# A linear-attention layer with key dimensions innermost, normalisation on GpSimd, biases as matmul rows, and its weights loaded in the layer before

## The chip, the cores and the metric

The kernel runs on one core of a Trainium2 chip. A core has a matrix engine (TensorE, "PE" in rows; its weight loads are "PEld"), VectorE ("DVE"), ScalarE ("ACT"), GpSimd ("POOL") and SyncE ("SP"), which here only issues transfers. Engines run their own instruction streams in order and wait for each other through semaphores. The metric is the device time of one execution in microseconds, lower is better. Before the change the median of 3 runs is 1361.99 us (1359.45 to 1362.17).

## The reference

Four layers over a sequence of 2048 rows of 128 floats, each added to x after a layer norm: softmax attention (16 heads), a layer of 8 experts with one expert per row, the linear attention that is edited here, and the expert layer once more. The linear attention:

```python
qkv = x @ w_qkv.T + b_qkv                   # x: layer-normed, (1, 2048, 128)
q, k, v = heads(qkv)                        # 16 heads of 8
q_prime, k_prime = elu(q) + 1, elu(k) + 1
kv_cumsum = cumsum(einsum('bhtd,bhte->bhtde', k_prime, v), axis=2)
context = einsum('bhtd,bhtde->bhte', q_prime, kv_cumsum)
norm = einsum('bhtd,bhtd->bht', q_prime, cumsum(k_prime, axis=2))
out = context / (norm[..., None] + 1e-6)
x = x + out @ w_out.T + b_out
```

## The kernel before, in words

x stays on the chip as 16 tiles of 128 rows (one row of the sequence per partition). The four layers are written one behind the other: `attention`, `ffn`, `linear_attention`, `ffn`. Each is one block with a barrier at its end, and its own PSUM and SBUF tiles.

`linear_attention` treats one tile per step. For tile t: normalise (`xn`, L1051, VectorE), transpose on TensorE (L1153) and copy by ScalarE (`xT`, L1098); one product gives q, k and v in PSUM (`z`, L1159), and a second one with a single row, `b_row` by `ones` in f32, adds the bias (L1160). ScalarE and VectorE make elu+1 of q and k (`qk`; "features", L1102, L1105, L1063); v with a column of ones behind each head is `v1`. GpSimd writes out the outer product of k and v1 for every row (`outer`, L1037: 16 heads x 8 key dimensions x 9 values = 1152 floats), TensorE sums it over the rows of the tile so far with a triangular matrix (`sums`, L1143, three products of 512, 512 and 128 columns). VectorE multiplies by q (`prod`, L1059) and sums over the 8 key dimensions (`own`, L1066). The order of the 1152 floats is head, key dimension, value, so that sum reads with a step of 9 floats.

What lies before the tile comes through a state. TensorE forms k^T v of the tile (`delta`, L1135), ScalarE copies it (`mine`, L1095), GpSimd masks it to the heads (`fresh`, L1027) and adds it to the running `state` (L1031); q^T against the state is `inter` (L1148). VectorE adds `inter` and `own` (`tot`, L1069), adds 1e-6 (L1071), takes the reciprocal (L1073) and multiplies (`o`, L1075). `o` is transposed (L1165), copied (`oT`, L1108), multiplied by the output weights (L1126) and added to x (L1056). The output bias is added to x earlier, by GpSimd (L1024). Buffers are doubled (U = 2).

Each engine's order is written out by `skewed`: at step n it emits its stages for tiles n - offset, in the order in which the table names them. TensorE: y (5), qT (2), z (1), xT (0), sums (2), oT (4). VectorE: norm (0) and y (5), heads (3), features (1), sums (2). The middle of it is a hardware loop with two tiles a turn. GpSimd: bias (0), outer (1), state (2). Weights and biases are loaded at the start of the layer (L995 to L998), transposed on TensorE (L1116, L1117) and copied (L1086).

`ffn` computes the expert of every row, gives the rows places sorted by expert, scatters them to memory by 16 indirect transfers that GpSimd issues (L720), and then goes through 24 slots of 128 rows. TensorE and VectorE stand still while the scatter is issued.

## Time and profile before

| | us |
|---|---|
| median of 3 runs | 1361.99 |
| the profiled execution | 1360.53 |
| its span | 1358.8 |
| attention, first expert layer up to its end | 0 to 1127.1 |
| linear attention | 1127.1 to 1246.4 |
| second expert layer | 1246.4 to 1358.8 |

| engine | busy us | share of the span |
|---|---|---|
| TensorE | 1173.5 | 86% |
| VectorE | 957.3 | 70% |
| ScalarE | 794.6 | 58% |
| GpSimd | 829.2 | 61% |

Busy shares are means over four layers with different limits, so for the linear layer its own stretch has to be read. A row "start, duration, engine, line, operation, out<-in" is one instruction or several merged ones (xN); in brackets stands how long the engine was idle before it and what it waited for. Matrix products in f32 run as several passes and show as x2. PEclk is the clock that TensorE was granted, as a share of 2.4 GHz.

### The profile page before, as it was taken

To read this page: it belongs to the slowest core of one execution; us is meant where nothing else is said; L and a number is where in the kernel's file an instruction comes from. 1 tells how busy PE (TensorE), PEld (TensorE's weight loads), DVE (VectorE), ACT (ScalarE), POOL (GpSimd) and SP (SyncE) were. 2 spreads that over 40 slices of the span, in tenths; PEclk is the share of its full clock that TensorE was granted. 3 is DMA by queue.
4 is the path that set the end of the run, shared out by engine and by line. 5 is a ranking of instruction groups with operands and counts; after the bars stand their busy time and mean duration, and the time that the engine had idled before them with its cause. 6 is when DMAs were issued, how large, how long until landed. Compare 5 with 4: busy or idle time off the path is not lost. (4 is left out here: it accounts for less than half of the span.)

```text
span 1358.8 us, 24424 instructions
## 1 busy us (share of the span) xinstructions
PE 1173.5 (86%) x7936; PEld 855.3 (63%) x7936; DVE 957.3 (70%) x2108; ACT 794.6 (58%) x2192; POOL 829.2 (61%) x813
## 2 busy tenths in 40 slices
PE   5999999999999999999999999999973585885285
PEld 4666667676767767676676667676753582443285
DVE  5878677867776786878677777867743355998254
ACT  6777576767757775766677576766721342322053
POOL 0675668757866775887576768757852443552433
PEclk9899999999999999999999999999995796998588
DMA  4950200200020011002000200200000221000023
GB/s 124 125 141 16 48 1 1 52 12 1 1 63 1 1 32 32 1 1 63 1 1 8 57 1 1 50 14 1 1 1 17 57 61 32 1 0 1 29 60 98
DMA packets 52689, 41.18 MB, mean 30 GB/s; under 512 B 14177, under 2 KB 41442, under 8 KB 52578
## 3 DMA queue, kind: packets, MB, share of 16 engines
q1 hardware_dynamic: 50018, 34.50, 11.9%
q0 software_dynamic: 2560, 5.26, 1.2%
q8 instruction: 62, 1.02, 0.3%
q14 instruction: 49, 0.40, 0.1%
HBM read 13.49 MB, written 9.48 MB: 17 GB/s over the span
## 5 line engine op out<-in xcount | busy, mean ns | idle before, releaser
L325 POOL TENSOR_SCALAR at_prob<-at_prob,at_scale 128x512 f32<-128x512 f32 (+1 forms) x480 | 656.2, 1383 | 5.6
L353 DVE TENSOR_REDUCE at_nmax<-at_ps 128x1 f32<-128x512 f32 (+3 forms) x640 | 375.9, 603 | 154.1 <-PE at_ps L519 150.5
L434 ACT ACTIVATE at_prob<-at_ps,at_nmax 128x512 f32<-128x512 f32 (+3 forms) x640 | 393.1, 623 | 44.6 <-DVE at_nmax L353 43.7
L530 PE MATMUL at_ps<-ident,at_prob 128*128 128x128 f32 x2176 | 328.7, 275 | 23.4 <-DVE at_probT L376 19.1
L530 PEld LDWEIGHTS at_ps<-ident,at_prob 128*128 128x128 f32 x2176 | 255.7, 140 | 110.5 <-issue 52.6
L516 PE MATMUL at_ps<-at_k_st,at_q_parts 128*128 128x512 f32 (+3 forms) x640 | 285.1, 445 | 6.1 <-ACT at_prob L434 3.6
L448 ACT ACTIVATE at_probT<-at_ps 128x512 f32<-128x512 f32 (+1 forms) x288 | 165.1, 573 | 212.2 <-PE at_ps L530 188.0
L545 PE MATMUL at_ps<-at_probT,at_v 128*64 128x256 f32 (+1 forms) x2304 | 270.1, 374 | 12.3 <-DVE at_probT L376 12.3
L519 PE MATMUL at_ps<-at_k_st,at_q_parts 128*128 128x512 f32 (+3 forms) x640 | 253.1, 396 | 0.0
L376 DVE COPY at_probT<-at_ps 128x512 f32<-128x512 f32 (+1 forms) x288 | 189.0, 656 | 68.1 <-PE at_ps L530 64.7
L545 PEld LDWEIGHTS at_ps<-at_probT,at_v 128*64 128x64 f32 x2304 | 155.2, 136 | 107.1 <-issue 48.5
L516 PEld LDWEIGHTS at_ps<-at_k_st,at_q_parts 128*128 128x128 f32 x640 | 122.2, 191 | 46.7 <-ACT at_prob L434 22.0
L434 ACT ACTIVATION_READ_ACCUMULATOR at_prob<-at_ps,at_nmax 128x1 f32 x640 | 131.1, 205 | 0.0
L519 PEld LDWEIGHTS at_ps<-at_k_st,at_q_parts 128*128 128x128 f32 x640 | 125.8, 197 | 1.3
L382 DVE TENSOR_SCALAR at_prob<-at_prob,at_scale 128x512 f32<-128x512 f32 (+1 forms) x160 | 93.0, 583 | 2.5 <-POOL at_scale L318 2.0
L727 POOL DMA_INDIRECT slots_out<-f_ys,f_back x48 | 47.2, 984 | 63.9 <-DVE f_ys L836 49.2
L866 ACT ACTIVATE f_hT<-f_ps,f_wfix 128x128 f32<-128x128 f32 x192 | 54.6, 370 | 34.1 <-PE f_ps L911 28.8
L306 POOL TENSOR_TENSOR at_gap<-at_low,at_nmax 128x8 f32<-128x8 f32 (+2 forms) x48 | 9.9, 206 | 93.8 <-DVE at_low L358 93.8
L720 POOL DMA_INDIRECT slots_in<-f_xn,f_pos_u x32 | 31.3, 980 | 55.7 <-DVE f_pos_u L811 46.6
L904 PE MATMUL f_ps<-ident,f_xs 128*128 128x128 f32 x48 | 14.2, 296 | 57.3 <-DMA f_xs<-slots_in 57.3
L1037 POOL TENSOR_TENSOR li_outer<-li_qk,li_v 128x1152 f32<-128x1152 f32 x16 | 35.5, 2220 | 44.1 <-DVE li_qk L1063 44.1
L316 POOL COPY at_scale<-at_rinv 128x4 f32<-128x4 f32 x16 | 3.0, 189 | 96.6 <-DVE at_rinv L364 96.6
(189 smaller groups left out, 1364.1 us busy)
## 6 DMA issues: line engine op xcount, KB each, us to landing
at_q_parts<-at_q_parts SPq DMA_DIRECT2D x64, 256.0 KB, 3.5
f_xs<-slots_in SPq DMA_DIRECT2D x48, 64.5 KB
slots_in<-zeros SPq DMA_DIRECT2D x2, 1536.0 KB, 19.4
wall<-in_L_ffn_w_dram SPq DMA_DIRECT2D x1, 2048.0 KB, 19.8
wall<-in_L_ffn_w_dram SPq DMA_DIRECT2D x4, 512.0 KB, 6.1
f_got<-slots_out SPq DMA_DIRECT2D x8, 256.0 KB, 3.6
out_dram<-x SPq DMA_DIRECT2D x4, 256.0 KB, 2.4
slots_out<-f_ys,f_back POOLq DMA_INDIRECT x48
```

Of the source, the lines that this page charges most:

```text
L325: pool.tensor_scalar(cols, cols, scale[:, k, u, c:c + 1], None, ALU.mult).then_inc(s_fix["pool"], 1)
L353: dve.tensor_reduce(nmax[:, j % 2, u % 4, c:c + 1], bank, AX.X, ALU.max, negate=True).then_inc(s_max, 1)
L376: dve.tensor_copy(probT[1][n % TURNED][:, 0:w], turn_ps[1][:, 0:w]).then_inc(s_probT[1], 1)
L382: dve.tensor_scalar(cols, cols, scale[:, k, u, c:c + 1], None, ALU.mult).then_inc(s_fix["dve"], 1)
L434: act.activation(prob[j % 2][u % 4][:, c * BANK:c * BANK + w], ring[use_of["score", p, u, c] % RING][:, 0:w], ACT.Exp, bias=nmax[:, j % 2, ...
L448: act.activation(probT[0][n % TURNED][:, 0:w], turn_ps[0][:, 0:w], ACT.Copy).then_inc(s_probT[0], 1)
L516: pe.matmul(bank[:, 0:w], q_hi[h][:, r * P:(r + 1) * P], keys, start=True, stop=False)
L519: pe.matmul(bank[:, 0:w], q_lo[h][:, r * P:(r + 1) * P], keys, start=False, stop=True).then_inc(s_score, 1)
L530: last = pe.transpose(turn_ps[h][:, b * P:(b + 1) * P], prob[j % 2][2 * i + h][:, t * P:(t + 1) * P], ident[:, :])
L545: last = pe.matmul(z_ps[part_of, to:to + w], v[:, t, part_of], probT[h][group(p, j, g) % TURNED][:, 2 * P * b:2 * P * b + w], start=t == 0 ...
L727: pool.indirect_dma_start(scratch_out[:, :], bass.IndirectOffsetOnAxis(ap=back[k][:, :], axis=0), ys[k][:, :], None).then_inc(s_store[k], 16)
L866: last = act.activation(hT[k][:, f, :], ps[2 + c % 2][:, f * P:(f + 1) * P], ACT.Gelu, bias=wfix[k][:, B1.start + f:B1.start + f + 1])
```

## The change

1. The outer product and `prod` are laid out head, value, key dimension: the 8 key dimensions are innermost, and the sum over them reads neighbours.
2. The normalisation moves from VectorE to GpSimd; GpSimd's addition of the output bias goes.
3. The output bias and the 1e-6 become extra products with a row of ones. All bias rows are held as F32R in two parts, the rounded value in row 0 and what the rounding lost in row 32 of a tile of 33 rows (`b_rows`), against `ones` of 33 rows; the rows between are zero. The z bias goes the same way.
4. The running sum of the state is kept in PSUM form: `past` = k^T v + identity x `mine` of the tile before. GpSimd only masks it (one instruction in place of two).
5. xT, qT and oT share one PSUM bank (`turn_ps`), with waits so that none is written while another is read; `past`, `inter` and `out` have banks of their own.
6. Loads, masks and transposed weights are made by `linear_setup` inside the first expert layer (`beside`), into tiles that stay.
7. The steps are written out straight, without the hardware loop; buffers are guarded by explicit waits.

VectorE, one step in the middle of the linear layer, before (`li_prod` the product with q, `li_own` the sum over key dimensions, `li_xn` the normalised tile, `li_qk` the features):

```order
L1051 TENSOR_SCALAR li_xn<-x,li_mv,li_rstd 128x128
L1056 TENSOR_TENSOR x<-li_yp,x 128x128
L1066 TENSOR_REDUCE li_own<-li_prod 128x144
L1069 TENSOR_TENSOR li_tot<-li_stp,li_own 128x144
L1071 TENSOR_SCALAR li_den<-li_tot 128x16
L1073 RECIPROCAL li_den<-li_den 128x16
L1075 TENSOR_TENSOR li_o<-li_tot,li_den 128x128
L1063 SCALAR_TENSOR_TENSOR li_qk<-li_zp,li_ex 128x256
L1059 TENSOR_TENSOR li_prod<-li_sums,li_qk 128x1152
```

and after:

```order
L1114 TENSOR_TENSOR x<-li_outp,x 128x128
L1128 TENSOR_REDUCE li_own<-li_prod 128x144
L1131 TENSOR_TENSOR li_tot<-li_interp,li_own 128x144
L1133 RECIPROCAL li_den<-li_tot 128x16
L1137 TENSOR_TENSOR li_o<-li_tot,li_den 128x128
L1125 SCALAR_TENSOR_TENSOR li_qk<-li_zp,li_ex 128x256
L1118 TENSOR_TENSOR li_prod<-li_sums,li_qk 128x1152
```

The normalisation and the addition of 1e-6 are gone; nothing else has moved.

TensorE, one step, before (`li_yp` holds oT and the output product, `li_stp` is `inter`):

```order
L1126 MATMUL li_yp<-li_wT,li_oT 128x128
L1131 MATMUL li_qTp<-ident,li_qk 128x128
L1159 MATMUL li_zp<-li_wT,li_xT 128x384
L1160 MATMUL li_zp<-li_b_row,li_ones 128x384
L1153 MATMUL li_xTp<-ident,li_xn 128x128
L1135 MATMUL li_qTp<-li_v,li_qk 128x144
L1143 MATMUL li_sums<-li_outer,li_upto 128x512 x2
L1143 MATMUL li_sums<-li_outer,li_upto 128x128
L1148 MATMUL li_stp<-li_state,li_qT 128x144
L1165 MATMUL li_yp<-ident,li_o 128x128
```

and after (`li_turnp` is the shared bank of the transposes):

```order
L1249 MATMUL li_zp<-li_wT,li_xT 128x384
L1250 MATMUL li_zp<-li_b_rows,li_ones 128x384
L1243 MATMUL li_turnp<-ident,li_xn 128x128
L1222 MATMUL li_pastp<-li_v,li_qk 128x144
L1224 MATMUL li_pastp<-li_mine,ident 128x144
L1232 MATMUL li_sums<-li_outer,li_upto 128x512 x2
L1232 MATMUL li_sums<-li_outer,li_upto 128x128
L1238 MATMUL li_interp<-li_state,li_qT 128x144
L1239 MATMUL li_interp<-li_b_rows,li_ones 128x144
L1254 MATMUL li_turnp<-ident,li_o 128x128
L1211 MATMUL li_outp<-li_wT,li_oT 128x128
L1212 MATMUL li_outp<-li_b_rows,li_ones 128x128
```

Three products are new (L1224, L1239, L1212); the order of the others is as before (qT, L1216, stands right ahead of the piece shown).

GpSimd, the first steps, before:

```order
L1037 TENSOR_TENSOR li_outer<-li_qk,li_v 128x1152
L1024 TENSOR_TENSOR x<-x,li_bo_all 128x128
L1037 TENSOR_TENSOR li_outer<-li_qk,li_v 128x1152
L1027 TENSOR_TENSOR li_fresh<-li_mine,li_block_mask 128x144
L1031 TENSOR_TENSOR li_state<-li_state,li_fresh 128x144
L1024 TENSOR_TENSOR x<-x,li_bo_all 128x128
L1037 TENSOR_TENSOR li_outer<-li_qk,li_v 128x1152
L1027 TENSOR_TENSOR li_fresh<-li_mine,li_block_mask 128x144
```

and after:

```order
L1103 TENSOR_TENSOR li_outer<-li_qk,li_v 128x1152
L1086 TENSOR_SCALAR li_xn<-x,li_mv,li_rstd 128x128
L1103 TENSOR_TENSOR li_outer<-li_qk,li_v 128x1152
L1092 TENSOR_TENSOR li_state<-li_mine,li_block_mask 128x144
L1086 TENSOR_SCALAR li_xn<-x,li_mv,li_rstd 128x128
L1103 TENSOR_TENSOR li_outer<-li_qk,li_v 128x1152
L1092 TENSOR_TENSOR li_state<-li_mine,li_block_mask 128x144
L1086 TENSOR_SCALAR li_xn<-x,li_mv,li_rstd 128x128
L1103 TENSOR_TENSOR li_outer<-li_qk,li_v 128x1152
```

The normalisation of tile n+1 stands behind the outer product of tile n and the state of tile n-1.

The diff, cut to its core:

```diff
@@ ffn
             def _(sp):
                 sp.dma_start(wred[:, :], w_red).then_inc(s_gin, 16)
                 sp.dma_start(wg[:, :], w_g).then_inc(s_wg, 16)
+                if beside:
+                    beside["sync"](sp)
                 sp.wait_ge(s_scat, 16 * NT)
...
             def _(pool):
                 pool.iota(xn[:, :, D:D + 1].bitcast(U32), pattern=[[P, NT], [0, 1]], base=0, channel_multiplier=1).then_inc(s_ids, 1)
+                if beside:
+                    beside["gpsimd"](pool)
...
                 dve.tensor_scalar(slot_e[:, :], slot_f[:, :], float(E - 1), None, ALU.min).then_inc(s_slot, 1)
+                if beside:
+                    beside["vector"](dve)
...
                 act.activation(ex[:, :, :], sub[:, :, :], ACT.Exp).then_inc(s_ex, 1)
+                if beside:
+                    beside["scalar"](act, ps[3])
...
+                if beside:
+                    pe.wait_ge(beside["tensor"](pe, ps[3]), 1)
@@ linear_setup (new)
+    def on_sync(sp):
+        sp.dma_start(w_nat[:, 0:3, :], w_qkv.rearrange("(a p) d -> p a d", p=P)).then_inc(s_in, 16)
+        sp.dma_start(w_nat[:, 3, :], w_out).then_inc(s_in, 16)
+        sp.wait_ge(s_clear, 3)
+        for r in (0, BROWS - 1):
+            sp.dma_start(b_nat[r:r + 1, 0:3 * D], b_qkv.unsqueeze(0)).then_inc(s_bias, 16)
+            sp.dma_start(b_nat[r:r + 1, 3 * D:4 * D], b_out.unsqueeze(0)).then_inc(s_bias, 16)
+    def on_vector(dve):
+        dve.wait_ge(s_c, 3)
+        dve.tensor_copy(ones[:, :], ones_f[:, :])
+        dve.wait_ge(s_bias, 64)
+        dve.wait_ge(s_clear, 3)
+        dve.tensor_copy(b_cut[:, :], b_nat[:, :]).then_inc(s_cut, 1)
+        dve.tensor_copy(b_rows[0:BROWS - 1, :], b_nat[0:BROWS - 1, :])
+        dve.wait_ge(s_cut, 1)
+        row = slice(BROWS - 1, BROWS)
+        dve.tensor_tensor(b_rows[row, :], b_nat[row, :], b_cut[row, :].bitcast(F32), ALU.subtract).then_inc(s_const, 1)
+    def on_tensor(pe, bank):
+        pe.wait_ge(s_in, 32)
+        for a in range(4):
+            last = pe.transpose(bank[:, a * P:(a + 1) * P], w_nat[:, a, :], ident[:, :])
+        last.then_inc(s_wTp, 1)
+        return s_wT
...
@@ linear_attention, GpSimd
+                    if stage == "norm":
+                        if t >= U:
+                            pool.wait_ge(s_xTp, t - U + 1)
+                        pool.tensor_scalar(xn[k][:, :], x[:, t, :], mv[:, t, 0:1], rstd[:, t:t + 1],
+                                           ALU.subtract, ALU.mult).then_inc(s_xn, 1)
...
-                        pool.tensor_tensor(state[k][:, :], state[1 - k][:, :], fresh[k][:, :], ALU.add).then_inc(s_state, 1)
+                        pool.tensor_tensor(state[k][:, :], mine[k][:, :], block_mask[:, :, :].rearrange("p h e -> p (h e)"),
+                                           ALU.mult).then_inc(s_state, 1)
...
-                        kk = qk[k][:, D:2 * D].rearrange("p (h d) -> p h d", d=DL).unsqueeze(3).to_broadcast([P, HL, DL, DL + 1])
-                        vv = v1[k][:, :, :].unsqueeze(2).to_broadcast([P, HL, DL, DL + 1])
+                        kk = qk[k][:, D:2 * D].rearrange("p (h d) -> p h d", d=DL).unsqueeze(2).to_broadcast([P, HL, DL + 1, DL])
+                        vv = v1[k][:, :, :].unsqueeze(3).to_broadcast([P, HL, DL + 1, DL])
                         pool.tensor_tensor(outer[k][:, :, :, :], kk, vv, ALU.mult).then_inc(s_outer, 1)
@@ VectorE
-                        dve.tensor_reduce(own[:, :, :], prod[:, :, :].rearrange("p (h d) e -> p h e d", d=DL), AX.X, ALU.add).then_inc(s_own, 1)
+                        dve.tensor_reduce(own[:, :, :], prod[:, :, :, :], AX.X, ALU.add).then_inc(s_own, 1)
...
-                        dve.tensor_scalar(den[:, :].unsqueeze(2), tot[:, :, DL:DL + 1], EPS, None, ALU.add).then_inc(s_den, 1)
-                        dve.wait_ge(s_den, t + 1)
-                        dve.reciprocal(den[:, :], den[:, :]).then_inc(s_rden, 1)
+                        dve.reciprocal(den[:, :].unsqueeze(2), tot[:, :, DL:DL + 1]).then_inc(s_rden, 1)
@@ TensorE
+                        pe.matmul(out, oT[k][:, :], wT[:, 3, :], start=True, stop=False)
+                        pe.matmul(out, ones[:, :], b_rows[:, 3 * D:4 * D], start=False, stop=True).then_inc(s_out, 1)
...
+                        last = pe.matmul(past, qk[k][:, D:2 * D], v1[k][:, :, :].rearrange("p h e -> p (h e)"), start=True, stop=t == 0)
+                        if t:
+                            last = pe.matmul(past, ident[:, :], mine[1 - k][:, :], start=False, stop=True)
+                        last.then_inc(s_past, 1)
...
+                            pe.matmul(inter, qT[k][:, :], state[1 - k][:, :], start=True, stop=False)
+                        pe.matmul(inter, ones[:, :], b_rows[:, 4 * D:4 * D + VX], start=t == 0, stop=True).then_inc(s_inter, 1)
...
-                        pe.matmul(z_ps[:, 0:3 * D], ones[:, :], b_row[:, :], start=False, stop=True).then_inc(s_z, 1)
+                        pe.matmul(z_ps[:, 0:3 * D], ones[:, :], b_rows[:, 0:3 * D], start=False, stop=True).then_inc(s_z, 1)
```

## Rows read from the trace of the kernel before

**Rows 1.** Table of stretches: us, busy us of each engine, granted clock, DMA.
```profile
1041.70:1065.50 23.80, 0.02 (x1) 0.02 (x1) 0.77 (x1) 0.00 (x0) 15.68 (x16) 0.50 0.16 49
1134.00:1147.50 13.50, 12.09 (x21) 5.16 (x22) 1.10 (x3) 2.78 (x11) 5.80 (x5) 0.50 0.00 0
1158.00:1239.00 81.00, 68.26 (x246) 35.20 (x246) 77.81 (x119) 23.32 (x87) 46.54 (x52) 0.98 0.00 0
```
**Rows 2.** Timeline, VectorE, one step: start us, duration us, what.
```profile
1190.26 1.35 DVE L1059 TENSOR_TENSOR li_prod<-li_sums,li_qk 128x1152 f32<-128x1152 f32 x1
1191.52 1.20 DVE L1051 TENSOR_SCALAR li_xn<-x,li_mv,li_rstd 128x128 f32 x1
1192.64 0.28 DVE L1056 TENSOR_TENSOR x<-li_yp,x 128x128 f32 x1
1192.85 2.21 DVE L1066 TENSOR_REDUCE li_own<-li_prod 128x144 f32<-128x1152 f32 x1
1195.16 0.31 DVE L1069 TENSOR_TENSOR li_tot<-li_stp,li_own 128x144 f32<-128x144 f32 x1
1195.50 0.17 DVE L1071 TENSOR_SCALAR li_den<-li_tot 128x16 f32<-128x16 f32 x1
1195.71 0.25 DVE L1073 RECIPROCAL li_den<-li_den 128x16 f32<-128x16 f32 x1
1196.20 0.42 DVE L1063 SCALAR_TENSOR_TENSOR li_qk<-li_zp,li_ex 128x256 f32<-128x256 f32 x1
```
**Rows 3.** Timeline, TensorE, the same step and the next y.
```profile
1190.23 0.49 PE L1126 MATMUL li_yp<-li_wT,li_oT 128*128 128x128 f32 x2 [0.37 <-ACT li_oT L1108]
1190.66 0.82 PE L1159 MATMUL li_zp<-li_wT,li_xT 128*128 128x384 f32 x2
1191.41 0.91 PE L1160 MATMUL li_zp<-li_b_row,li_ones 1*128 1x384 f32 x2
1192.78 0.33 PE L1153 MATMUL li_xTp<-ident,li_xn 128*128 128x128 f32 x1 [0.46 <-DVE li_xn L1051]
1193.20 2.10 PE L1143 MATMUL li_sums<-li_outer,li_upto 128*128 128x512 f32 x6
1195.52 0.51 PE L1148 MATMUL li_stp<-li_state,li_qT 128*128 128x144 f32 x2 [0.22 <-DVE li_tot L1069]
1195.87 0.27 PE L1165 MATMUL li_yp<-ident,li_o 128*128 128x128 f32 x1
1196.51 0.49 PE L1126 MATMUL li_yp<-li_wT,li_oT 128*128 128x128 f32 x2 [0.37 <-ACT li_oT L1108]
```
**Rows 4.** Line of the normalisation: count, ns minimum/median/maximum, first and last start.
```profile
L1051 DVE TENSOR_SCALAR li_xn<-x,li_mv,li_rstd x16: 337/1198/1204, 1132.1 to 1222.9; 128x128 f32<-128x128 f32 x8, 128x128 f32 x8
```
**Rows 5.** Timeline, GpSimd, the same step.
```profile
1190.42 2.22 POOL L1037 TENSOR_TENSOR li_outer<-li_qk,li_v 128x1152 f32<-128x1152 f32 x1 [2.56 <-DVE li_qk L1063]
1193.17 0.49 POOL L1031 TENSOR_TENSOR li_state<-li_state,li_fresh 128x144 f32<-128x144 f32 x1
```
**Rows 6.** Timeline, TensorE in the attention layer, an F32R product and its successor.
```profile
701.18 0.40 PE L519 MATMUL at_ps<-at_k_st,at_q_parts 128*128 128x512 f32 x1
701.42 0.60 PE L530 MATMUL at_ps<-ident,at_prob 128*128 128x128 f32 x4
```
**Rows 7.** Groups by line and shape, 300 to 1000 us: count, busy us, mean ns.
```profile
L325 POOL TENSOR_SCALAR at_prob<-at_prob,at_scale 128x128 f32<-128x128 f32 x46 | 27.5, 598 | 0.0
```
**Rows 8.** Timeline, the start of the linear layer: first transpose, first sums, second product.
```profile
1134.05 0.45 PE L1153 MATMUL li_xTp<-ident,li_xn 128*128 128x128 f32 x1 [3.10 <-ACT li_wT L1086]
...
1143.49 4.05 PE L1143 MATMUL li_sums<-li_outer,li_upto 128*128 128x512 f32 x6
...
1152.81 1.35 DVE L1059 TENSOR_TENSOR li_prod<-li_sums,li_qk 128x1152 f32<-128x1152 f32 x1
```
**Rows 9.** Timeline, the last product of the linear layer.
```profile
1238.08 1.35 DVE L1059 TENSOR_TENSOR li_prod<-li_sums,li_qk 128x1152 f32<-128x1152 f32 x1
```
**Rows 10.** Timeline, GpSimd, first scatter of the first expert layer.
```profile
1041.76 1.18 POOL L720 DMA_INDIRECT slots_in<-f_xn,f_pos_u  x1 [22.26 <-DVE f_pos_u L811]
```

More of the change, by code:

```diff
@@ L620, in static_tile, with ffn @@
     return c if isinstance(turn, int) else None
-def ffn(nc, shp, keep, tag, w_red, w_g, scratch_in, scratch_out, has_stats, out=None):
+def ffn(nc, shp, keep, tag, w_red, w_g, scratch_in, scratch_out, has_stats, out=None, beside=None):
     T, D, NT, NC, TPC = shp.T, shp.D, shp.NT, shp.NC, shp.TPC
@@ L934, in linear_attention @@
+def linear_attention(nc, shp, keep):
     D, NT = shp.D, shp.NT
@@ L1016, in _ @@
[L1016 to L1031 removed]
+                    pool.memset(v1[k][:, :, DL:DL + 1], 1.0).then_inc(s_one, 1)
@@ L1107, in emit @@
                         act.wait_ge(s_oTp, t + 1)
+                        if t >= U:
+                            act.wait_ge(s_out, t - U + 1)
                         act.activation(oT[k][:, :], oT_ps, ACT.Copy).then_inc(s_oT, 1)
-                skewed(act, NT, U, {"qT": 2, "z": 1, "xT": 0, "delta": 2, "oT": 4}, emit)
+                in_turn({"qT": 2, "z": 1, "xT": 0, "past": 2, "oT": 4}, emit)
             @block.tensor
             def _(pe):
-                pe.wait_ge(s_in, 32)
-                for a in range(3):
-                    pe.transpose(sums_ps[:, a * P:(a + 1) * P], w_nat[:, a, :], ident[:, :])
@@ L1127, in emit @@
                     elif stage == "qT":
                         pe.wait_ge(s_qk, t + 1)
-                        if not first(turn, c):
-                            pe.wait_ge(s_dcopy, t)
-                        pe.transpose(qT_ps[:, 0:P], qk[k][:, 0:D], ident[:, :]).then_inc(s_qTp, 1)
+                        turn_bank_free(t, "q")
+                        pe.transpose(qT_ps, qk[k][:, 0:D], ident[:, :]).then_inc(s_qTp, 1)
                     elif stage == "sums":
                         pe.wait_ge(s_v, t + 1)
-                        pe.wait_ge(s_qT, t + 1)
@@ L1137, in emit @@
+                        last.then_inc(s_past, 1)
                         pe.wait_ge(s_outer, t + 1)
-                        if not first(turn, c):
+                        if t:
                             pe.wait_ge(s_prod, t)
-                        flat = outer[k][:, :, :, :].rearrange("p h d e -> p (h d e)")
+                        flat = outer[k][:, :, :, :].rearrange("p h e d -> p (h e d)")
                         for a in range(0, OUTER, BANK):
@@ L1144, in emit @@
                         last.then_inc(s_sums, 1)
[L1145 removed]
+                        pe.wait_ge(s_qT, t + 1)
+                        if t:
                             pe.wait_ge(s_tot, t)
                             pe.wait_ge(s_state, t)
[L1148 removed]
+                            pe.matmul(inter, qT[k][:, :], state[1 - k][:, :], start=True, stop=False)
+                        pe.matmul(inter, ones[:, :], b_rows[:, 4 * D:4 * D + VX], start=t == 0, stop=True).then_inc(s_inter, 1)
                     elif stage == "xT":
                         pe.wait_ge(s_xn, t + 1)
[L1151 to L1153 removed]
+                        turn_bank_free(t, "x")
+                        pe.transpose(xT_ps, xn[k][:, :], ident[:, :]).then_inc(s_xTp, 1)
                     elif stage == "z":
                         pe.wait_ge(s_xT, t + 1)
[L1156 removed]
+                        if t:
                             pe.wait_ge(s_qk, t)
```

229 lines of the change are left out of this document (128 added, 101 removed).

## The prediction

> **What bounds the kernel now.** I read the table of stretches first [rows 1], to find what the edited part is worth: the linear layer runs from 1127.1 to 1246.4 us, 119 us of a span of 1358.8, and nothing else of the kernel is edited except a few instructions in the first expert layer. From 1158 to 1239 VectorE is busy 77.8 of 81.0 us and TensorE 68.3, at a granted clock of 0.98 (the 2.4 GHz level); GpSimd has 46.5 and waits. From 1134 to 1147.5 the granted clock is 0.50 (1.2 GHz). So the steady part is VectorE's, with TensorE close behind.
>
> The timeline of one step shows how. VectorE goes from one instruction to the next without a gap [rows 2]: product at 1190.26, normalisation 1191.52 (1.20 us), x add 1192.64, reduction 1192.85 (2.21), total, den, reciprocal, `o` (between the reciprocal and the features), features 1196.20. TensorE's final product (y) recurs at 1190.23 and 1196.51 [rows 3], so a step (one tile of 128 rows) is 6.28 us. TensorE waits 0.46 for xn, 0.22 for the total and 0.37 for oT in it.
>
> **VectorE, part by part.** The normalisation goes: it takes 337 ns where nothing runs beside it and 1198 in the median [rows 4]. In the shown step it ends at 1192.72, just behind GpSimd's outer product (1190.42 plus 2.22) [rows 5]: most of it is a wait for GpSimd. Start to start, from it to the x add, 1.12 us go. The den addition goes: 0.21 (1195.50 to 1195.71). The reduction reads 1152 elements with a step of 9 floats in 2.21 us; the product, also 1152 elements, contiguous, takes 1.35 [rows 2]. Its new form reads innermost runs of 8 contiguous floats. Bounds: 1.35 and 2.21, and I take 1.35, a saving of 0.86. VectorE then needs 6.28 - 1.12 - 0.21 - 0.86 = 4.09 us a step. It is no longer the bound.
>
> **TensorE, by start-to-start distances in [rows 3].** Present step 6.28. What changes:
> - z bias, one row of f32: 1191.41 to the end of its 0.91, about 0.75 of TensorE's time once hand-over is left off. Now F32R. The nearest row of an F32R product is 512 columns in 0.24 (701.18 to 701.42) [rows 6]; 384 columns lie between 0.1 and 0.24. I take 0.20: -0.55.
> - a second product for `past` (identity times the copied state, f32, 144 columns). The existing one of 144 columns and the transpose before it take 0.42 together (1192.78 to 1193.20); transpose 0.16: +0.26.
> - two more F32R products (eps into `inter`, bias into `out`), each between 0.1 and 0.24: 0.15 each, +0.30.
> - the stalls for xn and for the total go: -0.62 (1191.41 to 1192.78 is 1.37, of which 0.75 is work) and -0.28 (2.32 to the `inter` product, 2.04 unstalled). The 0.64 from oT to y (1195.87 to 1196.51) stays: transpose, ScalarE's copy, then y.
> Sum: 6.28 - 0.55 + 0.26 + 0.30 - 0.62 - 0.28 = 5.39 us. That is TensorE alone.
>
> **The loop that is late next.** GpSimd now has, in its order, normalisation(n+1) behind state(n-2) behind outer(n-1). The nearest row for a normalisation there is the 128x128 tensor-scalar, 0.60 us [rows 7]; outer 2.22, state 0.49 [rows 5]: 3.3 us a step, no bound by itself. But it stands in a loop over two steps: y start, to VectorE's x add 0.7 (0.49 of product, bias row, hand-over), x add 0.2, reduction 1.45, total 0.34, reciprocal and `o` 0.49 (1195.71 to 1196.20), features 0.42, outer with hand-over 2.28, state 0.54, normalisation 0.73, then TensorE: transpose 0.16, past 0.52, sums 2.04, inter and its eps row 0.45, oT to y 0.64. Sum 10.96 us, so 5.48 a step. This is a little above 5.39, and I take 5.5. Below: with a GpSimd normalisation of 0.34 as on VectorE and cheaper F32R rows it is 5.2. Above: with the reduction still at 2.21 it is (10.96 + 0.86)/2 = 5.9.
>
> The page "GPSIMD Engine Reference" of the Trainium skill (Key points) speaks against moving work to GpSimd: that engine shares its SBUF interface with VectorE, and VectorE collides with it in a two-port mode or with two SBUF inputs; elementwise work there is about half as fast. The trace agrees on the first (1198 against 337 ns) and on the second (0.60 against 0.34). By that rule `o`, which reads two SBUF tiles, could wait as the normalisation does now; what that would cost here is a rival below.
>
> **Start of the layer.** Statistics and table loads stay. Before: normalisation at 1132.11, first transpose only at 1134.05, as it stood behind the weights' transposes, copy and ScalarE's tables [rows 8]. After: normalisation on GpSimd 1132.1 to 1132.7, transpose 1132.8, 1.25 earlier. At half clock each of two z bias rows costs 1.5 before and 0.4 now: -2.2. Against it normalisation(2) stands behind outer(0), +0.6, and the second `past` product is not there yet; hand-overs +0.3. So the first `sums` starts at 1140.9 in place of 1143.49. It keeps 4.05 less its last hand-over, 3.8, and ends at 1144.7. Then inter, qT, z, bias, xT, past at full clock, 2.1, sums(1) 2.1: product(1) at 1148.95 in place of 1152.81, 3.9 earlier.
>
> **Middle and tail.** Product(1) to product(15) is 1238.08 - 1152.81 = 85.3 us in 14 intervals [rows 8, 9]. After: one of 5.0, eleven of 5.5, then 5.2 (no transpose of x) and 4.3 (no z): 75.0. Product(15) at 1223.95, 14.1 earlier. Behind it the shorter reduction and the missing den give 1.05: 15.2 in all.
>
> **Work moved to the first expert layer.** Six loads and a wait for the clearing on SP's queue stand ahead of its wait for the scatter; GpSimd gets ten fills and masks, VectorE three copies and a subtraction, TensorE four transposes, ScalarE one copy. GpSimd waits 22.26 us there for the positions [rows 10], and from 1041.7 to 1065.5 VectorE has one instruction and TensorE nothing [rows 1]; that hides all of it. Not hidden: the fills run beside VectorE's first normalisations, which can wait as in [rows 4], once, at most 0.86; and two copies beside GpSimd's scatter issue, between 0 and 0.5. I take +0.8 together. If the cover were gone it would be some 5 us, but queues of 22 us make that remote. The second expert layer, from 1246.4, only starts earlier.
>
> **Sum.** The profiled execution took 1360.53 us (span 1358.8). 1360.5 - 15.2 + 0.8 = 1346.1. The median of the runs shown is 1361.99, 1.5 above it; half of that goes to the forecast: **1347 us**.
>
> **Rivals.**
> 1. *The loop over GpSimd is looser.* Normalisation near 0.4, F32R rows near 0.1: a step of 5.2, TensorE alone. Eleven steps by 0.3 less are 3.3: 1343 to 1344. For: the 0.60 was taken beside a busy VectorE. Against: it is the only row of that size.
> 2. *VectorE stays slow*: the reduction does not gain from its layout, or `o` waits for GpSimd. The first gives 5.9 a step, 11 x 0.4 + 0.9 = 5.3 more: 1352. The second: counted from y's start, `o` begins near 3.0 (0.7, 0.2, 1.45, 0.34, 0.28), while the outer, state and normalisation of the step before end near 7.1 - 5.5 = 1.6, so they should not meet; if `o` waited 0.5 each step, half of it would show in the two-step loop, 11 x 0.25, about 1350.
> 3. *The clock rises later.* The half level lasted from 1134 to about 1147 while TensorE was nearly always busy. Now it has less to do there. Each further step at half clock costs TensorE's own work once more, about 4 us: 1351 for one step.
> 4. *Slower than before*: GpSimd's outer product dislikes runs of eight with the value broadcast innermost. It stands in the two-step loop, so the gain of 15 us is spent once a step grows by 1.25 (12 steps), that is when outer takes 2.22 + 2.5 = 4.7 us. At 5.5 us a step is 7.1 and the time 1366. For: it is the one large instruction whose operands' innermost steps change place. Against: it reads the same two kinds of step before, swapped; and even the slowest rate that a GpSimd row here has, 0.598 us for 128 elements, is 5.4 us for 1152 only if its fixed part grew with it.
> That the change does not do what it says is covered in 2.
>
> **Chances.** Forecast (1344 to 1350) 0.52; rival 1 0.15; rival 2 0.14; rival 3 0.11; rival 4 0.04; the rest (moved work exposed, a later stall in the shared transpose bank) 0.04, within 1350 to 1360. The range to hold 8 in 10: 1340 to 1354. A measurement of this kernel tells about 0.2%, 2.7 us, from no change: faster 0.94, same 0.02, slower 0.04.
>
> **What would show it.** Reduction rows near 1.35 and no normalisation on VectorE (right) or 2.2 (rival 2); steps of 5.5 between products, with VectorE idle ahead of its x add and TensorE waiting a little for xn from GpSimd (the loop), none of it (rival 1); outer still 2.2; F32R rows under 0.25; first `sums` at 14 us after the layer's start and clock at the 2.4 GHz level by the second; from the first to the second expert layer's start 15 us less. The forecast is wrong if TensorE shows a wait not named here, most likely on the bank that xT, qT and oT share, or if the first expert layer grows by more than 1 us.

## The result, and the profile after

The changed kernel takes 1353.84 us (median of 5 runs, 1352.68 to 1355.14) against 1361.99 (5 runs, 1358.84 to 1362.51): ratio 0.9949, interval 0.9934 to 0.9965. It is faster by 8.15 us; 15 were forecast. The profiled execution took 1353.84 us with a span of 1352.1.

By layer: the linear layer now runs from 1127.24 (first statistics) to 1238.38 (first statistics of the next layer), 111.14 us in place of 119.29: -8.15, forecast -15.2. The first expert layer, which got the set-up, is less than 0.1 us longer (forecast +0.8). The second one, which nothing edits, is 1.3 us longer in this profile (1238.38 to the end, 113.7, against 112.4). The granted clock goes with it: it is 0.50 (the 1.2 GHz level) from 1234.1 to 1295.6 here, 61 us, and was from 1243.4 to 1298.1, 55 us, before. Of the fifteen profiles of this document, the nine in which this stretch lasts 55 us have a second expert layer of 111.7 to 112.4 us, and the six in which it lasts 58 or 61 us one of 113.5 to 114.1. What makes it longer is not shown, so the 1.3 us are not counted as an effect of the change.

One step on TensorE, changed kernel (start, duration, operation; compare [rows 3]):
```profile
1186.32 0.49 PE L1211 MATMUL li_outp<-li_wT,li_oT 128*128 128x128 f32 x2 [0.37 <-ACT li_oT L1179]
1186.74 0.32 PE L1212 MATMUL li_outp<-li_b_rows,li_ones 33*128 33x128 f32 x1
1186.99 0.33 PE L1216 MATMUL li_turnp<-ident,li_qk 128*128 128x128 f32 x1
1187.16 0.81 PE L1249 MATMUL li_zp<-li_wT,li_xT 128*128 128x384 f32 x2
1187.90 0.43 PE L1250 MATMUL li_zp<-li_b_rows,li_ones 33*128 33x384 f32 x1
1188.27 0.33 PE L1243 MATMUL li_turnp<-ident,li_xn 128*128 128x128 f32 x1
1188.43 0.41 PE L1222 MATMUL li_pastp<-li_v,li_qk 128*128 128x144 f32 x2
1188.68 0.41 PE L1224 MATMUL li_pastp<-li_mine,ident 128*128 128x144 f32 x2
1188.92 2.10 PE L1232 MATMUL li_sums<-li_outer,li_upto 128*128 128x512 f32 x6
1190.86 0.41 PE L1238 MATMUL li_interp<-li_state,li_qT 128*128 128x144 f32 x2
1191.20 0.33 PE L1239 MATMUL li_interp<-li_b_rows,li_ones 33*128 33x144 f32 x1
1191.46 0.33 PE L1254 MATMUL li_turnp<-ident,li_o 128*128 128x128 f32 x1
1192.16 0.49 PE L1211 MATMUL li_outp<-li_wT,li_oT 128*128 128x128 f32 x2 [0.37 <-ACT li_oT L1179]
```
The step is 1192.16 - 1186.32 = 5.84 us, and the one wait in it is the 0.37 for oT, which was there before. The waits for xn and for the total are gone.

The same step on VectorE and GpSimd (compare [rows 2, 5]):
```profile
1187.10 0.29 DVE L1114 TENSOR_TENSOR x<-li_outp,x 128x128 f32<-128x128 f32 x1 [0.52 <-PE li_outp L1212]
1187.31 1.34 DVE L1128 TENSOR_REDUCE li_own<-li_prod 128x144 f32<-128x1152 f32 x1
...
1191.06 1.36 DVE L1118 TENSOR_TENSOR li_prod<-li_sums,li_qk 128x1152 f32<-128x1152 f32 x1 [1.05 <-PE li_sums L1232]
```
```profile
1186.87 0.80 POOL L1086 TENSOR_SCALAR li_xn<-x,li_mv,li_rstd 128x128 f32<-128x128 f32 x1
```
The table of stretches over twelve steps (compare [rows 1]; busy of PE, PEld, DVE, ACT, POOL, then the granted clock):
```profile
1158.00:1226.00 68.00, 63.96 (x258) 37.11 (x257) 47.70 (x83) 20.70 (x82) 37.52 (x33) 1.00 0.00 1
```
TensorE is busy 94% of it, VectorE 70% (before, 84 and 96%). VectorE idles 0.52 + 1.05 us a step, each time for TensorE. The reduction went from 2.21 to 1.34 as forecast; the outer product is 2.17; the normalisation on GpSimd takes 0.80 where I had 0.60.

The start of the layer on TensorE (compare [rows 8]):
```profile
1140.78 0.48 PE L1243 MATMUL li_turnp<-ident,li_xn 128*128 128x128 f32 x1 [0.66 <-POOL li_xn L1086]
...
1141.53 4.02 PE L1232 MATMUL li_sums<-li_outer,li_upto 128*128 128x512 f32 x6
...
1153.23 0.33 PE L1243 MATMUL li_turnp<-ident,li_xn 128*128 128x128 f32 x1 [1.69 <-POOL li_xn L1086]
```
TensorE waits twice here for the moved normalisation, 0.66 and 1.69 us. From 1145.58 the products on VectorE (its multiplication by q, `li_prod`, one for each tile) start at intervals of 4.23, 6.23, then 5.84 eleven times, 5.77 and 4.56.

### The profile page after: what moved, and what is told of

The parts are those of the page before. It is cut to its first block and busy times, and to the rows that moved or that the text cites. A ratio compares the mean times of both kernels' runs of the same rounds, so it can differ in the third digit from the quotient of the medians.

```text
span 1352.1 us, 24428 instructions
## 1 busy us (share of the span) xinstructions
PE 1178.1 (87%) x7980; PEld 864.7 (64%) x7980; DVE 930.6 (69%) x2080; ACT 794.5 (59%) x2192; POOL 829.7 (61%) x798
## 3 DMA queue, kind: packets, MB, share of 16 engines
q0 software_dynamic: 2560, 5.26, 1.2%
```

## The experiments

Theory T: in the changed kernel TensorE alone sets the step, since its short bias products cost more than I gave them; next behind it is the two-step loop over GpSimd. Theory G: that loop sets it. All edits are to the changed kernel unless said otherwise. Where two steps are given, they alternate. What stands ahead of the linear layer scatters by execution (it starts at 1127.1 to 1131.7 us in the 15 profiles), so beside the medians I compare the layer's own span:

| run | layer, us | step, us | median, us | ratio to before, interval |
|---|---|---|---|---|
| before | 119.29 | 6.28 | 1361.99 | |
| changed | 111.14 | 5.84 | 1353.84 | 0.9934 to 0.9965 |
| e_norows | 101.46 | 5.03/5.48 | 1343.84 | 0.9866 to 0.9899 |
| e_double | 112.46 | 5.95 | 1353.93 | 0.9942 to 0.9975 |
| e_ot | 103.47 | 5.25/5.39 | 1347.22 | 0.9888 to 0.9921 |
| e_layout | 105.44 | 5.36 | 1349.88 | 0.9895 to 0.9936 |
| e_past | 110.70 | 5.64/5.87 | 1354.62 | 0.9930 to 0.9965 |
| e_norm | 106.68 | 5.84 | 1349.23 | 0.9895 to 0.9928 |
| e_oldlay | 116.77 | 5.84/6.21 | 1360.83 | 0.9989 to 1.0008 |
| e_early | 107.17 | 5.84 | 1350.92 | 0.9905 to 0.9938 |
| e_f32rows | 115.62 | 6.17 | 1358.12 | 0.9969 to 0.9992 |
| e_rows128 | 101.81 | 4.85/5.75 | 1344.73 | 0.9861 to 0.9894 |
| e_best3 | 100.77 | 5.37 | 1343.54 | 0.9852 to 0.9884 |
| e_best1 | 91.25 | 4.53 | 1333.95 | 0.9790 to 0.9818 |
| e_best4 | 90.65 | 4.53 | 1333.17 | 0.9783 to 0.9816 |

**e_norows.** The products for b_out and 1e-6 are left out, and with them that part of the computation.
```diff
-                        pe.matmul(out, oT[k][:, :], wT[:, 3, :], start=True, stop=False)
-                        pe.matmul(out, ones[:, :], b_rows[:, 3 * D:4 * D], start=False, stop=True).then_inc(s_out, 1)
+                        pe.matmul(out, oT[k][:, :], wT[:, 3, :], start=True, stop=True).then_inc(s_out, 1)
...
-                            pe.matmul(inter, qT[k][:, :], state[1 - k][:, :], start=True, stop=False)
-                        pe.matmul(inter, ones[:, :], b_rows[:, 4 * D:4 * D + VX], start=t == 0, stop=True).then_inc(s_inter, 1)
+                            pe.matmul(inter, qT[k][:, :], state[1 - k][:, :], start=True, stop=True).then_inc(s_inter, 1)
```
(For the first tile the product of 1e-6 stays.)


> The changed kernel without the added product for the output bias and without the one for 1e-6 (both are left out of the computation). Theory T (TensorE alone sets the step of 5.84 us, and each short F32R product costs 0.25 to 0.35 us of it): the step falls by 0.6 to about 5.25, some 8 us in all, 1346. Rival G (the two-step loop over GpSimd's normalisation sets it): the loop as measured in the changed kernel is 11.2 us for two steps, 5.6, and loses only 0.3 a step; a step of 5.3 with TensorE waiting for xn. If the F32R products cost what the forecast said (0.15 each): 5.54 and 1349.

The layer lost 9.7 us. The two products were worth more than the 0.30 I had given them: the step is 5.26 in the mean. It alternates, since the loop of theory G ends last in every second one:
```profile
1182.41 0.41 PE L1237 MATMUL li_interp<-li_state,li_qT 128*128 128x144 f32 x2
1182.66 0.27 PE L1254 MATMUL li_turnp<-ident,li_o 128*128 128x128 f32 x1
...
1185.29 0.33 PE L1243 MATMUL li_turnp<-ident,li_xn 128*128 128x128 f32 x1 [0.38 <-POOL li_xn L1086]
```
The mean of 5.26 doesn't separate the theories, for T had given 5.25 and G 5.3 with a wait for xn. But the steps in which TensorE does not wait for xn price the two products: 5.03 in place of 5.84, so 0.41 each. From y to the next transpose it is 0.32 (1183.30 to 1183.62) in place of 0.67, from `inter` to the transpose of o 0.25 in place of 0.60, and the distance behind each of these transposes is 0.06 shorter.

**e_double.** The b_out product is done twice, so that bias is added twice.


> The changed kernel with the output-bias product issued twice (the bias is added twice). It prices one more F32R product right behind another. If what costs is the change from f32 to F32R and back, a step grows by 0.06 to 0.1 us, 1 to 1.5 us in all. If every such product costs 0.25, it grows by 0.25, some 4 us, 1358. Under rival G less than half of either shows.


```profile
1187.42 0.49 PE L1211 MATMUL li_outp<-li_wT,li_oT 128*128 128x128 f32 x2 [0.37 <-ACT li_oT L1179]
1187.84 0.33 PE L1212 MATMUL li_outp<-li_b_rows,li_ones 33*128 33x128 f32 x1
1188.01 0.27 PE L1213 MATMUL li_outp<-li_b_rows,li_ones 33*128 33x128 f32 x1
1188.21 0.33 PE L1217 MATMUL li_turnp<-ident,li_qk 128*128 128x128 f32 x1
```
The step grew by 0.11 only. From y to the next transpose it was 0.67 us with one bias product and 0.79 with two; before the change, without one, 0.32 (1190.23 to 1190.55). So the first costs 0.35 there and a second beside it 0.12: most of the price is for the change from one sort of product to the other, not for the columns.

**e_ot.** oT has its place in the bank of `out`, and TensorE transposes o ahead of the sums, so that ScalarE (its table is edited in the same way) copies it meanwhile.
```diff
-in_turn({"y": 5, "qT": 2, "z": 1, "xT": 0, "sums": 2, "oT": 4}, emit)
+in_turn({"y": 5, "qT": 2, "z": 1, "xT": 0, "oT": 4, "sums": 2}, emit)
```


> The changed kernel with the transpose of o ahead of the sums (in the output bank instead of the shared one), so that ScalarE's copy lies beside the sums and the output product need not wait for it. Theory T: the 0.37 us wait and its hand-over go from every step, 5.84 to about 5.4, 6 to 7 us in all, 1347. Rival G: the loop loses about 0.27 a step, 5.6 to 5.3, so it would allow the same. If something else bounds the step (VectorE), no change: 1353.8.

The only TensorE wait of the steady step goes, and the step falls by that and a little more, to 5.32 in the mean. This doesn't separate T from G either: the loop of G got shorter too, and 5.3 was what it allowed. It does show that VectorE isn't the bound.

**e_layout.** The kernel before, with the new order of elements alone (outer, product, reduction).


> The kernel before with only the new layout (key dimensions innermost in outer, prod and the sum); normalisation on VectorE, biases, loads and loop as before. By theory T the layout alone takes VectorE's step from 6.28 to 5.42, and TensorE without the added products needs 5.38: a step of 5.4 to 5.5, shorter than in the changed kernel; 9 to 11 us less than before, 1351 to 1353, although the start of the layer gains nothing. If the layout is worth little by itself: 1358 to 1362.


```profile
1184.34 1.15 DVE L1051 TENSOR_SCALAR li_xn<-x,li_mv,li_rstd 128x128 f32 x1
1185.61 1.34 DVE L1067 TENSOR_REDUCE li_own<-li_prod 128x144 f32<-128x1152 f32 x1
```
VectorE is still without a gap, and the step is 5.36: this one part of the change gives 13.9 us of layer, the whole change 8.2. The rest of the change costs more on TensorE than it frees. The median, 1349.88, is 1 us below what was expected. (This layer started 4.5 us later than before the change, behind unedited code; the timed runs spread from 1345.3 to 1351.2.)

**e_past.** The masked state is summed on GpSimd as before; no identity product.


> The changed kernel (1353.8 us, step 5.84), but the masked state is summed on GpSimd as before (two instructions there in place of one), and TensorE has no identity product for past. Theory T (TensorE's own instructions set the step of 5.84): TensorE loses the 0.25 us of that product and would come to 5.59; GpSimd's two-step loop, 11.2 us in the changed kernel, grows by about 0.25 to 0.3, 5.7 to 5.75 a step, and now ends last. Step 5.6 to 5.75, 1350.5 to 1352.5 us. Rival G (the two-step loop over GpSimd already sets 5.84): the step grows to 5.95 or more, 1355 to 1357.

The later steps have a mean of 5.75, at the upper end of what T gave: GpSimd's second instruction (0.49 us) is paid in the loop. The time is 2 us above what T gave, 1354.62. Most of that is the interval from the second to the third product, 7.84 in place of 6.23. TensorE waits 2.63 us for xn in it (1.69 in the changed kernel), and then the granted clock falls back to the 1.2 GHz level for a while:
```profile
1154.45 0.33 PE L1249 MATMUL li_turnp<-ident,li_xn 128*128 128x128 f32 x1 [2.63 <-POOL li_xn L1087]
...
1156.00:1159.00 3.00, 3.00 (x8) 1.56 (x6) 1.02 (x1) 0.00 (x0) 2.25 (x4) 0.50 0.00 0
```
The changed kernel has 1.00 over the same 3 us. So this run doesn't price the identity product in the time: in the later steps it costs 0.09 (5.84 for 5.75), and the layer without it is 0.4 us shorter.

**e_norm.** The normalisation back on VectorE, ahead of the x add.


> The changed kernel, but the normalisation is back on VectorE, ahead of the x add. Theory T: TensorE's 5.84 stays, VectorE gets 1.15 us (most of it waiting for GpSimd's outer product) where it idles 1.57 a step: step 5.84 to 5.95, 1353.5 to 1355.5 us. Rival G (GpSimd's loop sets the step): 0.8 us of it go every two steps, step 5.45, 1348 to 1349.

The step stays at 5.84, as T says, so G falls, though the time, 1349.23, is the one that G gave. The layer loses 4.5 us: I had looked at steps alone, and nearly all of it is at the start. The third product comes 24.9 us into the layer in place of 28.8. VectorE normalises in 0.34 for the first tiles, and TensorE's longest wait for xn there is 0.41. In the steady step it takes 0.46, since it starts at 1188.32, when GpSimd's outer product is over (1188.25).

**e_oldlay.** The old order of elements in the changed kernel.


> The changed kernel with the old element order in outer, product and reduction. The reduction takes 2.2 in place of 1.34 us. Theory T by TensorE alone: VectorE has 1.57 us idle a step and takes it, step 5.84, 1354 us. But the reduction also stands in the two-step loop over GpSimd (11.2 us + 0.86, 6.03 a step): by T with that loop as the next bound, step 6.0, 1356 to 1357. Rival V (VectorE still sets the step in the changed kernel): step 6.7, 1364 or more.

Mean step 6.02: the longer reduction is hidden where TensorE ends last (5.84), and shows in the loop (11.2 + 0.86 for two steps, 6.03). The time was 4 us above what I gave: the start lost 1.65 too (second to third product, 7.88), and there too the granted clock is 0.50 from 1156.3 to 1159.7, behind a wait of 2.19 us for xn. Without the new order the other edits together give nothing in the time; in the layer they give 2.5 us.

**e_early.** One line: GpSimd normalises one step further ahead.
```diff
-in_turn({"norm": 0, "outer": 1, "state": 2}, emit)
+in_turn({"norm": 0, "outer": 2, "state": 3}, emit)
```


> The changed kernel with one line edited: on GpSimd the normalisation of a tile stands one step further ahead of the outer product, so that no transpose of x has to wait for an outer product. This opens the two-step loop and changes nothing on TensorE. Theory T: step stays 5.84; only the one interval at the start that waited 1.69 us for xn gets shorter, at most 0.5: 1353 to 1354. Rival G: step 5.5 or less, 1349.


```profile
1142.30 2.54 PE L1232 MATMUL li_sums<-li_outer,li_upto 128*128 128x512 f32 x6
```
Step 5.84 again: G falls. But the layer is 4.0 us shorter, where I gave 0.5. The two waits of the start are gone (0.66 and 1.69), and the granted clock is at the 2.4 GHz level sooner. Windows of the changed kernel and of this one (stretch, busy of PE, PEld, DVE, ACT, POOL, granted clock, DMA share, GB/s):
```profile
1143.00:1145.00 2.00, 2.00 (x4) 0.73 (x3) 0.00 (x0) 0.00 (x0) 1.95 (x3) 0.50 0.00 0
1145.00:1147.00 2.00, 2.00 (x8) 1.01 (x6) 1.38 (x2) 0.28 (x1) 0.00 (x0) 0.90 0.00 0
```
```profile
1143.00:1145.00 2.00, 2.00 (x7) 0.96 (x5) 0.12 (x1) 0.00 (x0) 1.94 (x1) 0.96 0.00 0
```
0.90 over 1145 to 1147 puts the rise at 1145.4, 18.2 us into the layer; 0.96 over 1143 to 1145 puts it at 1143.2, 14.4 into the later start of this one. In between the first sums took 4.02 us in one and 2.54 in the other. The other profiles say the same: with GpSimd's old order the rise comes 17.3 to 17.7 us into the layer (e_norows, e_double, e_ot, e_past, e_oldlay, e_f32rows, e_rows128), without that wait 13.6 to 14.3 (e_norm, e_best1, e_best3, e_best4).

**e_f32rows.** The b_out and 1e-6 products as one row of f32.
```diff
-                        pe.matmul(out, ones[:, :], b_rows[:, 3 * D:4 * D], start=False, stop=True).then_inc(s_out, 1)
+                        pe.matmul(out, li["ones_f"][0:1, :], li["b_nat"][0:1, 3 * D:4 * D], start=False, stop=True).then_inc(s_out, 1)
...
-                        pe.matmul(inter, ones[:, :], b_rows[:, 4 * D:4 * D + VX], start=t == 0, stop=True).then_inc(s_inter, 1)
+                        pe.matmul(inter, li["ones_f"][0:1, :], li["b_nat"][0:1, 4 * D:4 * D + VX], start=t == 0, stop=True).then_inc(s_inter, 1)
```


> The changed kernel with two of its three bias products, the one of b_out (128 columns) and the one of 1e-6 (144 columns), as one row of f32 each in place of F32R; the one of z stays F32R. Theory S (a short F32R product between f32 ones is paid for its change of kind, not for its columns): in f32 they cost by columns, a third of the 0.75 us that 384 columns took before, 0.25 and 0.28, against 0.35 and 0.25 as F32R; step 5.75 to 5.85, 1352.5 to 1354 us, so F32R has gained nothing on them. Rival R (F32R is cheaper per column at this size too): the step grows by 0.2 or more, 1356 or more.


```profile
1189.21 0.49 PE L1211 MATMUL li_outp<-li_wT,li_oT 128*128 128x128 f32 x2 [0.37 <-ACT li_oT L1179]
1189.63 0.48 PE L1212 MATMUL li_outp<-li_b_nat,li_ones_f 1*128 1x128 f32 x2
1190.04 0.33 PE L1216 MATMUL li_turnp<-ident,li_qk 128*128 128x128 f32 x1
```
Slower by 0.33 a step: theory S falls and rival R holds, F32R is the cheaper kind by 0.16 to 0.18 a product. y is still followed after 0.42, as it was by the F32R product, though both products are f32 now; so a change of kind is not what delays the product behind y. What both forms share is that they have fewer rows (33 or 1) than their neighbours (128).

**e_rows128.** The bias rows stay F32R but get 128 rows, 126 of them zero.
```diff
-    BROWS = 33
+    BROWS, SECOND = P, 96
```
(The second part of a bias stands in row 96, `SECOND`, in place of row 32, and `ones` has 128 rows too.)


> The changed kernel with its three F32R bias products on 128 rows (126 of them zero) in place of 33: same kind, same columns, other height. Theory H (the price is a change of height between products of 128 rows and ones of 33 or 1): the product ahead of a bias row loses its 0.09 to 0.2 us, each bias product costs 0.12 to 0.17 as the second one did when it was doubled, step 5.84 - 0.35 to 0.5 = 5.35 to 5.5, 1348 to 1350 us. Theory K (the price is the change between f32 and F32R): nothing changes, 5.84, 1354 us.


```profile
1180.81 0.49 PE L1211 MATMUL li_outp<-li_wT,li_oT 128*128 128x128 f32 x2 [0.37 <-ACT li_oT L1179]
1181.06 0.31 PE L1212 MATMUL li_outp<-li_b_rows,li_ones 128*128 128x128 f32 x1
1181.20 0.30 PE L1216 MATMUL li_turnp<-ident,li_qk 128*128 128x128 f32 x1
1181.33 0.81 PE L1249 MATMUL li_zp<-li_wT,li_xT 128*128 128x384 f32 x2
1181.68 0.64 PE L1250 MATMUL li_zp<-li_b_rows,li_ones 128*128 128x384 f32 x1
1182.16 0.28 PE L1243 MATMUL li_turnp<-ident,li_xn 128*128 128x128 f32 x1
...
1185.66 0.49 PE L1211 MATMUL li_outp<-li_wT,li_oT 128*128 128x128 f32 x2 [0.37 <-ACT li_oT L1179]
...
1187.86 0.33 PE L1243 MATMUL li_turnp<-ident,li_xn 128*128 128x128 f32 x1 [0.69 <-POOL li_xn L1086]
...
1190.46 0.41 PE L1238 MATMUL li_interp<-li_state,li_qT 128*128 128x144 f32 x2
1190.61 0.32 PE L1239 MATMUL li_interp<-li_b_rows,li_ones 128*128 128x144 f32 x1
1190.77 0.28 PE L1254 MATMUL li_turnp<-ident,li_o 128*128 128x128 f32 x1
```
Theory H holds, and by more than I gave. From y to the next transpose 0.39 in place of 0.67; from z to the transpose of x 0.83 in place of 1.11; from `inter` to the transpose of o 0.31 in place of 0.60; the transposes behind them get shorter too (0.11 in place of 0.16 from xT to `past`). A step without a wait for xn, 1180.81 to 1185.66, is 4.85 in place of 5.84: 0.99 us for three products, 0.33 each. That is TensorE alone. The loop over GpSimd is now the bound, with its 0.69 in every second step (4.85/5.75, mean 5.30). Nothing but the height of three products changed (with their weights, `ones`), and the layer lost 9.3 us.

The weight loads show where the time lies. Changed kernel, behind the y of 1186.32, and e_rows128, behind the y of 1180.81:
```profile
1186.74 0.18 PEld L1212 LDWEIGHTS li_outp<-li_b_rows,li_ones 33*128 33x128 f32 x1
```
```profile
1181.03 0.19 PEld L1212 LDWEIGHTS li_outp<-li_b_rows,li_ones 128*128 128x128 f32 x1
```
The weights of the 33 rows come 0.42 after y's start, together with their product, and those of 128 rows 0.22 after it; the load behind them follows after 0.25 (1186.99) and 0.13 (1181.16). So time is lost ahead of the low product and once more behind it. A bias product of 128 rows costs about 0.08 us (4.85 here, with z's on 128 rows as well, against 5.03 in e_norows, which has two fewer: 5.03 - 0.33 + 0.15), and one of 33 rows 0.41.

The page "TensorEngine Tiling (Array Packing)" of the Trainium skill (Key Properties) says: "Mode switching requires drain: Changing tiling mode (not just tile) drains the TensorE". These runs agree with it, if a product of 33 rows or of 1 counts as one of a smaller mode than 128, which no row here states: 0.33 us for going there and back is an estimate of that price from these runs. The page "TensorE: Matmul & The Clock Gate" of the Trainium skill (Why this matters for your kernels) adds that a single product of 32 rows takes as long as one of 128. Among products of 128 rows that does not hold here: the one of 33 rows costs 0.33 us more.

**e_best1, e_best3, e_best4.** The versions that the runs point to. e_best1: oT ahead; b_out added to x on GpSimd and 1e-6 on VectorE as before the change; normalisation on GpSimd one step further ahead. e_best3: the same with the normalisation on VectorE, ahead of the x add. e_best4: e_best1 with the z bias on 128 rows.


> The changed kernel with what the runs point to: oT transposed ahead of the sums, no product for b_out (GpSimd adds it to x, as before the change), no product for 1e-6 (VectorE adds it, as before the change), and the normalisation on GpSimd one step earlier. The F32R bias of z, the new order of elements, the identity product and the set-up in the first expert layer stay. By theory T TensorE alone needs 5.26 less the two waits seen there (0.19 in the mean, 0.37) = 4.7 us, VectorE 4.5, GpSimd 3.7, and no loop is over 4.8: step 4.75 to 4.9, linear layer 93 to 95 us, 1335 to 1338. Rival G (another loop through GpSimd's outer product sets the steps): step 5.2, 1341 or more.

> As the one with oT ahead and both bias products gone, but the normalisation on VectorE ahead of the x add, where it took 0.26 to 0.34 us in the earlier run with it there. TensorE 4.7, VectorE 4.5 + 0.3 = 4.8 us a step: 4.8 to 4.95, linear layer 92 to 95, 1334 to 1338 us. If at this shorter step the normalisation meets GpSimd's outer product, it takes 1.1 as before the change, step 5.6, 1344.

> The fastest version so far (step 4.53 us, 1334 us), with its one F32R product, the bias of z, on 128 rows in place of 33. Theory H: 0.1 us less on TensorE a step; VectorE has 0.1 idle a step there, so step 4.45 and 1332.5 to 1334 us. Theory K: no change, step 4.53, 1334 us.

e_best1 takes 1333.95 us, 0.9804 of the time before the change and 20 us below the changed kernel. It came out 1 us under the range that I gave, since the step is 4.53. e_best3 ended at its rival's 1344: at this step VectorE's normalisation meets GpSimd's outer product again (0.92 in place of 0.34) and TensorE waits 0.69 for it:
```profile
1188.11 0.92 DVE L1118 TENSOR_SCALAR li_xn<-x,li_mv,li_rstd 128x128 f32<-128x128 f32 x1
```
```profile
1189.08 0.33 PE L1248 MATMUL li_turnp<-ident,li_xn 128*128 128x128 f32 x1 [0.69 <-DVE li_xn L1118]
```
e_best4 freed TensorE (it waits 0.23 a step for VectorE now), but the step did not move from 4.53. I had expected 4.45; its 1333.17 can't be told from 1333.95. The step alone would fit theory K, but the distance from z to the transpose of x fell from 1.11 to 0.82, as H says.
```profile
1185.56 1.36 DVE L1127 TENSOR_TENSOR li_prod<-li_sums,li_qk 128x1152 f32<-128x1152 f32 x1
1186.84 0.28 DVE L1123 TENSOR_TENSOR x<-li_outp,x 128x128 f32<-128x128 f32 x1
1187.26 0.30 PE L1259 MATMUL li_outp<-ident,li_o 128*128 128x128 f32 x1 [0.23 <-DVE x L1123]
1187.95 2.10 PE L1236 MATMUL li_sums<-li_outer,li_upto 128*128 128x512 f32 x6
1189.53 0.42 DVE L1134 SCALAR_TENSOR_TENSOR li_qk<-li_zp,li_ex 128x256 f32<-128x256 f32 x1
1190.09 1.36 DVE L1127 TENSOR_TENSOR li_prod<-li_sums,li_qk 128x1152 f32<-128x1152 f32 x1
```
What holds it is a loop over both engines: product with q 1.28, x add 0.42 up to the transpose of o, that transpose and the two products of `past` 0.69, sums up to the next product with q 2.14, together 4.53. VectorE's own work is not the bound: its features end at 1189.95, the sums at 1190.05, and the product starts right behind these (1190.09). e_best1 goes round the same loop in the same 4.53 (the product of 1185.62 there stands behind an idle 0.15 that ends with the sums). The transpose of o waits for the x add because both now use the bank of `out`, an edit that came with e_ot. Whether the x add ahead of the product with q would shorten it was not tried.

## Why the prediction was wrong, point by point

- **VectorE's part: right.** Reduction 1.34 (I took 1.35), normalisation and den gone, its own work 4.27 us (I had 4.09), no longer the bound. e_layout and e_oldlay show that the new order of elements alone carries the whole gain in time.
- **TensorE's sum, the step that failed.** It is the price of the F32R bias products: "I take 0.20" for z and "0.15 each" for the other two. I scaled the one F32R row at hand [rows 6] down by its columns, and overlooked that it is a product of 128 rows among others of 128, while these have 33. In place z's bias takes 0.37 to its successor (1187.90 to 1188.27), and the other two cost 0.41 each (e_norows): 0.69 more together. The rest of the sum was 0.24 too high: the sums give way to `inter` after 1.94 in place of 2.04, `inter` alone takes 0.25 where I counted the stalled 0.35, and small ones make the rest. 5.39 + 0.69 - 0.24 = 5.84, as measured: the sum erred on both sides, and the two errors cancel in part. The forecast itself went by the loop's 5.5, since 5.39 lay under it; with the measured prices TensorE ends last. e_double, e_f32rows and e_rows128 show that the height is what costs; the kind (0.16 to 0.18 a product) and the columns (0.37 at 384, 0.25 at 128, to the successor) come behind it, and F32R is the cheaper kind. With 128 rows the same program's step on TensorE is 4.85, below my 5.39.
- **The loop over GpSimd: mechanism right, not the bound.** I had 10.96 us for two steps (with `inter` and its 1e-6 product at 0.45, where TensorE's sum had 0.50); with 0.80 for the normalisation it is 11.2, 5.6 a step, under TensorE's 5.84. It shows as soon as TensorE is relieved (e_norows, e_rows128) or the loop lengthened (e_past, e_oldlay, 6.02 for 6.03).
- **The start: half right.** First sums at 1141.53 (forecast 1140.9), but product(1) at 1149.81 in place of 1148.95, and the next interval 6.23 in place of 5.0. I had counted "normalisation(2) stands behind outer(0), +0.6", and not that normalisation(3) stands behind outer(1) and (2). e_early and e_norm show that the place of the normalisation behind GpSimd's outer product costs about 4 us here. In e_early 2.35 of them are the two waits; the other 1.6 go with the earlier rise of the clock (the first sums alone are 1.48 shorter), and no run moves the clock by itself.
- **Account of the 7.1 us missing in the layer:** product(1) relative to the layer's start 0.7, the next interval 1.2, eleven steps by 0.34 3.7, the last two intervals 0.8, the tail 0.5 (7.80 from product(15) to the end, where I had 8.33 - 1.05). So about 2 us are the start, and 5 the dearer products: where two of them are left out (e_norows) the last two intervals and the tail are 4.96, 3.76 and 6.58, under what I gave.
- **Work in the first expert layer:** under 0.1 us in place of +0.8 in the profile. The 13 profiles with it start the linear layer at 1127.1 to 1130.6, the two without at 1127.1 and 1131.7, so a cost of under a few us isn't settled.
- **Rivals.** The time lies 2 to 4 us above those of rivals 2 and 3 (1350 to 1352), and just inside the range of 1340 to 1354, but neither rival happened: the reduction gained, `o` takes its 0.29, the clock rose at 1145.4, before the second tile's sums. That the time is inside the wide range is no merit of the mechanism. Rival 4's outer product kept its 2.17.

## What to carry to other kernels

Before short products are put on TensorE to relieve another engine, look at the height of their neighbours: a bias product of 33 rows among products of 128 cost 0.41 us here (128 or 144 columns), one of 128 rows, 126 of them zero, about 0.08. When an engine that was the bound falls to 70% busy and the step hardly moves, read the next engine's start-to-start distances; the edit that freed the first one (here the order of elements) may be worth more alone. Before the next engine is relieved in its turn, follow the loop between engines too: in e_best4 both engines have time left in a step (TensorE 0.23 us, VectorE 0.14) and it stands still at 4.53. Work moved to a slow in-order engine has to be issued ahead of its long instruction, at the start of the pipeline above all.
